# Adapter and expert FFN on one Trainium2 core: the opening reordered in two halves

## The reference

```
hidden = gelu(x @ down_W.T + down_b)                       # 512 -> 128
Wsel, bsel = expert_W[id0], expert_b[id0]
expert_out = hidden @ Wsel.T + bsel
hidden = where(valid, expert_out, hidden) + domain_emb[id0]
x1 = layernorm(hidden @ up_W.T + up_b + x) * ln_gamma + ln_beta
h = gelu(x1 @ Wi[id1] + bi[id1])                           # 512 -> 2048
y = layernorm(h @ Wo[id1] + bo[id1] + x1) * gamma[id1] + beta[id1]
```

## Time and profile before

| what | value |
|---|---|
| median of 3 runs | 781.45 us (781.15 to 781.71) |
| the profiled execution | 781.23 us |
| its span in the trace | 779.4 us |
| PE busy | 762.1 us, 98% |
| DVE, POOL, ACT busy | 516.7, 466.2, 347.4 us |
| DMA | 45.70 MB, mean 59 GB/s |
| PE busy from 60 us to the end | 707.52 of 719.40 us |

### The profile page before, as it was taken

How to read it: one execution, slowest core, us unless ns; L and a number is a source line. 1 busy time by engine, 2 the same in 40 slices (tenths; PEclk the granted TensorE clock), 3 DMA queues, 4 the chain that set the end, 5 groups by cost and what they waited for, 6 DMA issues and landing times.

```text
span 779.4 us, 10642 instructions
## 1 busy us (share of the span) xinstructions
PE 762.1 (98%) x3418; PEld 631.0 (81%) x3418; DVE 516.7 (66%) x1064; ACT 347.4 (45%) x601; POOL 466.2 (60%) x401
## 2 busy tenths in 40 slices
PE   8999999999999999999999999999999999999996
PEld 7878887888878888788887888878887888888885
DVE  6676874678556894578837798277874778646115
ACT  3454445434445344534445444444445434443432
POOL 5766654675647756386644855548654676646444
PEclk9999999999999999999999999999999999999999
DMA  9930000310012000137212200022000110001001
GB/s 325 407 126 1 1 0 1 122 41 0 1 56 82 27 1 1 70 115 276 81 55 68 95 0 1 3 95 68 1 1 1 64 45 1 0 12 43 1 0 54
DMA packets 17049, 45.70 MB, mean 59 GB/s; under 512 B 2274, under 2 KB 2530, under 8 KB 16098
## 3 DMA queue, kind: packets, MB, share of 16 engines
q1 hardware_dynamic: 16274, 43.67, 15.4%
q10 hardware_dynamic: 720, 1.31, 0.6%
HBM read 36.59 MB, written 8.39 MB: 58 GB/s over the span
## 4 chain that ended last, share of the span: by engine, by line
PE 91%; DVE 4%; issue 2%; ACT 1%; DMA 1%; POOL 0%; ACTq 0%; DVEq 0%; POOLq 0%
PE acc L751 15%; PE acc L753 15%; PE acc L752 14%; PE ps_h L751 14%; PE ps_h L753 14%; PE ps_h L752 14%; PE ps L751 2%; PE ps L753 2%; PE ps L752 2%; DVE xt L525 1%; DVE rows L607 1%; DMA xt_raw<-in_xT 1%; ACT ps_h L434 1%; PE ps_h L823 0%; DVE x1t L590 0%
## 5 line engine op out<-in xcount | busy, mean ns | idle before, releaser
L274 POOL TENSOR_TENSOR wi<-w_raw,wi 128x512 fp32r<-128x512 f32 x128 | 165.4, 1293 | 257.0 <-ACT wi L418 256.9
L433 ACT ACTIVATE h<-ps_h,bi_now 128x512 fp32r<-128x512 f32 x126 | 86.9, 690 | 372.3 <-PE ps_h L753 372.2
L595 DVE TENSOR_TENSOR h<-ps_h,h 128x512 fp32r<-128x512 f32 x126 | 87.0, 691 | 198.5 <-ACT ps_h L434 197.6
L751 PE MATMUL acc<-wo,h 128*128 128x512 f32 x512 | 199.2, 389 | 0.0
L752 PE MATMUL acc<-wo,h 128*128 128x512 f32 x512 | 199.2, 389 | 0.0
L753 PE MATMUL acc<-wo,h 128*128 128x512 f32 x512 | 199.2, 389 | 0.0
L751 PE MATMUL ps_h<-x1t,wi 128*128 128x512 f32 (+1 forms) x512 | 197.7, 386 | 0.4 <-DVE x1t L590 0.2
L752 PE MATMUL ps_h<-x1t,wi 128*128 128x512 f32 (+1 forms) x512 | 197.5, 386 | 0.0
L753 PE MATMUL ps_h<-x1t,wi 128*128 128x512 f32 (+1 forms) x512 | 197.5, 386 | 0.0
L280 POOL TENSOR_TENSOR wo<-w_raw,wo 128x512 fp32r<-128x512 f32 x128 | 165.9, 1297 | 7.1 <-ACT wo L424 7.1
L584 DVE STREAM_TRANSPOSE ps<-rows 32x128 f32<-32x128 f32 x448 | 144.2, 322 | 5.7
(11 more groups left out here) (129 smaller groups left out, 584.6 us busy)
## 6 DMA issues: line engine op xcount, KB each, us to landing
w_raw<-in_w SPq DMA_DIRECT2D x32, 512.0 KB, 8.5
rows<-in_x SPq DMA_DIRECT2D x32, 256.0 KB, 2.8
out<-rows SPq DMA_DIRECT2D x32, 256.0 KB, 2.0
xt_raw<-in_xT SPq DMA_DIRECT2D x7, 1024.0 KB, 4.8
vec<-in_vec SPq DMA_DIRECT2D x2, 768.0 KB, 10.7
xt_raw<-in_xT ACTq DMA_DIRECT2D x4, 256.0 KB, 6.1
vec<-in_vec SPq DMA_DIRECT2D x1, 512.0 KB, 6.6
down_raw<-in_down ACTq DMA_DIRECT2D x1, 256.5 KB, 2.7
```

The lines of the kernel that those rows point to most:

```text
L274: pool.tensor_tensor(slot[:, 1], w_raw[:, c, 0, :].rearrange("p (k i) -> p k i", k=KD), slot[:, 0].bitcast(F32), ALU.subtract).then_inc(wi ...
L433: act.activation(h[:, c % H_RING, 0, :], bank, ACT.Gelu, bias=bias)
L595: dve.tensor_tensor(h[:, c % H_RING, 1, :], hidden_bank(t, c), h[:, c % H_RING, 0, :].bitcast(F32), ALU.subtract).then_inc(h_split, 1)
L751: pe.matmul(out, left[0], right[0], start=start, stop=False)
```

## The change

Everything lies in the opening, but for one item (the fold of the second sequence).

- **Two halves.** `xt_raw` is loaded in four pieces j, each two chunks k of 256 columns (rows of x): j = 0, 1 are the first 256 rows, j = 2, 3 the last. Pieces 2 and 3 are issued after ACT's table load and first gelu. `first_down(j)` is 6 matmuls of 256 columns; j = 0, 1 go to `ps0` bank 0, j = 2, 3 to bank 1, later. `first_hidden` and `first_hid_rest` work on 256 columns. The rests of pieces 0 and 1 are DVE's (`first_rest`), those of 2 and 3 POOL's; so `xt_split`, on which SP waits before it issues the next tile's `xt_raw`, now comes from POOL.
- **Expert.** ACT makes the hi part (scale = valid), DVE the rest in one operation; identity * (1 - valid) is a matrix of its own (`exp_off`, kept in a corner of `fold_w`), and `fold_product` has 5 matmuls rather than 3, for both sequences. ACT makes `exp_b`. POOL computes `valid`. The fold of sequence 0 goes into a `ps_h` bank.
- **Down weights.** Both parts by DVE (before: DVE and POOL).
- **Residuals** of s = 0, 1 by one fp32 matmul each with the identity (`first_residual`); their norms one after the other rather than as a pair.
- **keep_warm** only once, 11 matmuls.
- **Order.** `first_down(2)`, `(3)` and two bias products stand before `turn(0)`; `adapter_up` of s = 2, 3 behind `turn(0)` and `turn(1)`. On POOL the four `wi_rest` come before the last two `inverse_root`; `add_out_bias(0)` moves into c = 1 to 4 of tile 0. The first two `xt_round`/`xt_rest` of tile 1 come before the first gelus. `vec0` is loaded before the first `w_raw`. The copy of `bi` for tile 0 is gone.

```diff
-WARM = (14, 1, 12, 6)
+WARM = 11
...
+        exp_off = [fold_w[:, b, 1, 0:A] for b in range(BATCH)]
...
+        def fold_bank(b):
+            return ps0[:, 1, :] if b else ps_h[:, 0, :]
+        def half(j):
+            return slice(j // 2 * HALF, (j // 2 + 1) * HALF)
+        def pair(j):
+            return slice(j % 2 * 2, j % 2 * 2 + 2)
...
+            sp.dma_start(vec0[:, :, :], vec0_d[:, 1:3, :].to_broadcast([P, 2, D])).then_inc(vec0_landed, 16)
             load_w(0, 0)
-            sp.dma_start(vec0[:, :, :], vec0_d[:, 1:3, :].to_broadcast([P, 2, D])).then_inc(vec0_landed, 16)
...
             pool.wait_ge(up_b_landed, 16)
-            for s in range(SUB):
-                add_up_bias(0, 1, s, 0)
+            add_up_bias(0, 1, 0, 0)
+            add_up_bias(0, 1, 1, 0)
+            first_rest(2)
+            first_rest(3)
             inverse_root(0, 0, 0)
+            add_up_bias(0, 1, 2, 0)
             inverse_root(0, 0, 1)
+            add_up_bias(0, 1, 3, 0)
             wi_rest(0, 0)
             wi_rest(0, 1)
+            wi_rest(0, 2)
+            wi_rest(0, 3)
             inverse_root(0, 0, 2)
             inverse_root(0, 0, 3)
-            wi_rest(0, 2)
-            wi_rest(0, 3)
...
-            for k in range(KD):
-                act.dma_start(xt_raw[:, k, :], xT_d[0, :, k, :]).then_inc(xt_first[k], 16)
+            for j in (0, 1):
+                act.dma_start(xt_raw[:, pair(j), half(j)], xT_d[0, :, pair(j), half(j)]).then_inc(xt_first[j], 16)
             act.wait_ge(const_ready, 2)
             act.activation(warm[:, :], neghalf[:, :], ACT.Gelu)
+            for j in (2, 3):
+                act.dma_start(xt_raw[:, pair(j), half(j)], xT_d[0, :, pair(j), half(j)]).then_inc(xt_first[j], 16)
...
+            first_round(0)
+            first_round(1)
             act.wait_ge(up_landed, 16)
             act.activation(up_w[:, 0, :], up_raw, ACT.Copy).then_inc(up_w_hi, 1)
-            act.wait_ge(down_landed, 16)
-            hidden(0)
+            expert_round()
+            first_expert_bias()
+            first_hidden(0, half_hi)
             fold_round(0)
+            first_round(2)
+            first_round(3)
             wi_round(0, 0, 0)
+            first_hidden(2, hid_hi)
             wi_round(0, 0, 1)
             x1t_round(0, 0, 0)
+            wi_round(0, 0, 2)
             x1t_round(0, 1, 0)
...
             x1t_round(0, 3, 0)
+            xt_round(1, 0)
+            xt_round(1, 1)
             for c in range(EARLY):
                 gelu(0, c, 0)
...
+            first_stats(0)
+            first_var(0)
             dve.wait_ge(vec0_landed, 16)
-            adapter_rows(0, (0, 1), 0, acc_part)
+            first_center(0)
+            first_stats(1)
+            first_scale(0)
+            first_var(1)
+            first_center(1)
+            first_hid_rest(2, hid_hi, hid_split)
+            first_scale(1)
             adapter_sum(0, 2, 0, acc_part(2))
...
+            def first_residual(s):
+                pe.wait_ge(xb_ready, s + 1)
+                pe.matmul(acc[:, s, :], ident[:, :], rows[:, 0, s, :], start=False, stop=False)
...
-                three(ps0[:, 1, :], [exp_w[:, i, :] for i in (0, 1)], [up_w[:, i, :] for i in (0, 1)],
-                      True, True).then_inc(fold_done, 1)
+                three(fold_bank(b), [exp_w[:, i, :] for i in (0, 1)], [up_w[:, i, :] for i in (0, 1)], True, False)
+                pe.matmul(fold_bank(b), exp_off[b], up_w[:, 0, :], start=False, stop=False)
+                pe.matmul(fold_bank(b), exp_off[b], up_w[:, 1, :], start=False, stop=True).then_inc(fold_done, 1)
...
-            keep_warm(WARM[0], ps_h[:, 1, :])
+            keep_warm(WARM, ps_h[:, 1, :])
             pe.wait_ge(down_w_ready, 1)
-            for k in range(KD):
-                adapter_down(0, k)
-            keep_warm(WARM[1], ps_h[:, 1, :])
+            first_down(0)
+            first_down(1)
             fold_product(0)
...
-            keep_warm(WARM[2], ps_h[:, 1, :])
+            first_down(2)
+            first_down(3)
+            bias_product(0, acc[:, 2, :], alone=False)
+            bias_product(0, acc[:, 3, :], alone=False)
             turn(0)
+            adapter_up(0, 0, 2, acc[:, 2, :], alone=False)
             turn(1)
-            keep_warm(WARM[3], ps_h[:, 1, :])
+            adapter_up(0, 0, 3, acc[:, 3, :], alone=False)
```

More of the change, by code:

```diff
@@ L328, in _ @@
[L328 to L332, removed]
+            pool.wait_ge(ids_all_landed, 16)
+            step(pool.tensor_scalar(valid[:, 0, :], ids_all[:, :], 0.0, None, ALU.is_ge))
+            step(pool.tensor_scalar(valid[:, 1, :], ids_all[:, :], float(E0), None, ALU.is_lt))
@@ new lines, in _, with first_rest @@
+            step(pool.tensor_tensor(valid[:, 0, :], valid[:, 0, :], valid[:, 1, :], ALU.mult))
+            step(pool.tensor_scalar(valid[:, 1, :], valid[:, 0, :], -1.0, 1.0, ALU.mult, ALU.add))
+            pool.sem_inc(valid_ready, 1)
+            pool.tensor_scalar(exp_off[0], ident[:, :], valid[:, 1, 0:1], None, ALU.mult).then_inc(exp_off_ready, 1)
+            def first_rest(j):
+                pool.wait_ge(xt_hi, j + 1)
+                part = x1t[1][:, :, pair(j), half(j)]
+                pool.tensor_tensor(part[:, 1], xt_raw[:, pair(j), half(j)], part[:, 0].bitcast(F32),
+                                   ALU.subtract).then_inc(xt_split, 1)
@@ L426, in gelu @@
             def gelu(t, c, parity):
-                if c == 0:
-                    act.wait_ge(bi_now_ready, t + 1)
+                first = isinstance(t, int) and t == 0
+                if c == 0 and first:
+                    act.wait_ge(bi_landed[0], 16)
+                elif c == 0:
+                    act.wait_ge(bi_now_ready, t)
                 act.wait_ge(mm1_done, CH * t + c + 1)
-                bias = bi_now[:, parity, c:c + 1]
+                bias = bi[:, 0, c:c + 1] if first else bi_now[:, parity, c:c + 1]
                 bank = hidden_bank(t, c)
@@ L460, in tile @@
                         x1t_round(t + 1, SPLIT_AT.index(c), 1 - parity)
-                    if more and c in (0, 1):
+                    if more and c in (0, 1) and not (isinstance(t, int) and t == 0 and c == 0):
                         xt_round(t + 1, 2 * c)
@@ L658, in expert_bias @@
                 dve.tensor_tensor(exp_b[:, 1, :], wide, exp_b[:, 0, :].bitcast(F32), ALU.subtract).then_inc(exp_b_ready, 1)
[L661 to L665, removed]
-            dve.wait_ge(down_landed, 16)
-            dve.tensor_copy(down_w[:, 0, :, :], chunks(down_raw[:, 0:D])).then_inc(down_w_hi, 1)
-            for k in range(KD):
-                xt_rest(0, k)
+            dve.wait_ge(down_landed, 16)
+            step(dve.tensor_copy(down_w[:, 0, :, :], chunks(down_raw[:, :])))
+            dve.tensor_tensor(down_w[:, 1, :, :], chunks(down_raw[:, :]), down_w[:, 0, :, :].bitcast(F32),
+                              ALU.subtract).then_inc(down_w_ready, 1)
+            first_rest(0)
+            first_rest(1)
             dve.wait_ge(up_w_hi, 1)
             dve.tensor_tensor(up_w[:, 1, :], up_raw, up_w[:, 0, :].bitcast(F32), ALU.subtract).then_inc(up_w_ready, 1)
-            dve.wait_ge(valid_ready, 1)
-            expert_bias(0)
-            hid_rest(0)
+            dve.wait_ge(exp_hi, 1)
+            expert_rest(0)
+            dve.wait_ge(first_split, 2)
+            dve.sem_inc(xt_split, 2)
+            first_hid_rest(0, half_hi, half_split)
             fold_rest(0)
```

152 lines of the change are left out of this document (103 added, 49 removed).

## The result

The changed kernel takes 777.32 us (median of 6 runs, 776.74 to 777.95) against 781.58 us (6 runs, 780.7 to 781.77): ratio 0.9946, 95% interval 0.9936 to 0.9956. The forecast was 776.9 and "faster". The profiled execution took 776.74 us with a span of 774.9, 4.5 under the 779.4 of before: the sum of the prediction to the tenth. Some of that is luck, as this execution is the fastest of its six; the medians are 4.26 us apart.

A forecast was written before the change was run, and what follows sets the result against it. PE's own work bounds the kernel from 60 us on, a latency chain the opening; 3.85 + 1.1 - 0.46 = 4.5 us off the profiled 781.23 gives 776.7, at the median 776.9. Own range 776.0 to 777.9; 80% range 775.8 to 779.6.

The forecast's parts named there:

- To the fold: Opening up to sequence 0's fold: PE begins at 6.6 us, `exp_w` is ready at 10.0, the fold runs to 11.4.
- First two subtiles: Adapter products of subtiles 0 and 1 after the fold: residual matmul 0.95 us each, subtile 1 done at 16.1.
- a price of nothing: POOL's rests of pieces 2 and 3, from 13.1 to 15.6 us, cost nothing because PE is still on subtile 1.
- Turns and start: Transposes and first FFN products: early products at 22.15 us, second halves at 29.2 instead of 33.05, a gain of 3.85.
- the stall for `wi_rest`: PE's wait for POOL's third `wi_rest` in the opening; done at 23.6 us, wanted at 25.05, so the stall goes.
- Behind it: After the opening: tile 1's first two `xt_rest` ahead of the gelus remove PE's stall at 44.02, worth 1.1 us.
- Given back: The second fold has two matmuls more on PE's path, which costs 0.46 us.
- tight but inside: POOL's added operations in c = 1 to 4 of tile 0: 5.1 us against 5.5 us of PE, so they fit.
- The clock did fall: Rival: PE's clock is low when real work starts, slow to 13 us; gain 1.5 us, time 780; 15%.
- the third rival: With fewer fillers the clock falls or stays down through the whole adapter: 9 us lost, time 786; 6%.
- The second half was not late: Rival: the second half or DVE comes later, 2 us late giving a gain of 2.5 to 3, time 778.7; 12%.
- no weight held the products: Rival: late weights hold the first FFN products, so there is no change, 781 to 782; 5%.

The follow-up runs named there:

- a_dve_rest: Changed kernel with the rests of pieces 2 and 3 of x on DVE instead of POOL: 777.41 us, 0.9948 of the kernel before.
- the two order experiments: POOL's last two `wi_rest` put ahead of the last two roots in the kernel before (779.79 us), and back behind them in the changed kernel (779.58 us).
- b_xt_early: Kernel before with only tile 1's first two `xt_round`/`xt_rest` moved ahead of tile 0's first gelus: 781.52 us, ratio 1.0002.
- a_fold1: Changed kernel with the second sequence's fold as before (three matmuls, identity part added by DVE): 782.52 us, 1.0023 of the kernel before.
- a_xt_late: Changed kernel with tile 1's first two roundings and rests put back behind the gelus: 778.27 us, 0.996 of the kernel before.
- a_wi_order: Changed kernel with POOL's last two `wi_rest` put back behind the last two roots: 779.58 us, 0.9973 of the kernel before.
- a_warm10: Changed kernel with 10 filler matmuls instead of 11, nothing else: 783.63 us, 1.0023 of the kernel before.
- a_fold1_pad: Changed kernel with the second fold as before (as in a_fold1) and 12 fillers instead of 11: 785.01 us, 1.0042 of the kernel before.
- a_warm0: Changed kernel without any filler matmuls: 777.96 us, 0.9955 of the kernel before.
- a_both: Changed kernel with the shorter second fold, 14 fillers and tile 0's `add_out_bias` moved ahead of the tile loop: 776.48 us, 0.9937 of the kernel before.

## Why the prediction was right, step by step

- **To the fold.** Piece 1 landed at 7.70 (forecast 7.73), piece 0 only at 6.24 instead of 5.24. So PE began at 7.74, not 6.6, and its long idle stretch (1.11 us) lies ahead of its first product, not behind it; the chain does not go through it. The two unknown 128x128 steps, taken as 0.3 each, took 0.41 and 0.36. `exp_w` was ready at 10.3, forecast 10.0. This is nearly all of the error in the opening.
- **First two subtiles.** The plain fp32 residual, bounded by 0.23 and 1.0 and taken as 0.95, took 0.98 and 0.86 in the chain. The upper bound was the right neighbour: the same kind of matmul. Subtile 1 ended at 16.36 (16.1). POOL's rests of pieces 2 and 3 ended at 15.9, ahead of that, as said, and a_dve_rest confirms a price of nothing. The Trainium skill (GPSIMD Engine Reference, Performance versus the Vector engine) speaks for VectorE here; it did not decide, although its ratio held (2.51 for POOL's two, 1.28 for DVE's two in a_dve_rest).
- **Turns and start.** The first turn began at 19.03 (18.8), the second was over by 20.52 (20.4), start at 22.30 (22.15), the last scale ended at 27.20 (27.15), second halves at 29.33 (29.2). The gain there is 3.7, forecast 3.85. Of it 2.05 is the earlier start and 1.65 the stall for `wi_rest`, which the two order experiments measured from both sides (1.64 and 1.68). The halves themselves, with the expert's new operations, were not undone by themselves: that they give the earlier start is read from the marks of the chain, and of the parts only the residual matmuls (0.7) and the fillers (1.0) were measured.
- **Behind it.** The early rests of tile 1 were put at 1.1; undoing them cost 1.16. My reason, an idle engine, was right, but the engine is idle only because POOL's additions and the copy of `bi` had moved away (b_xt_early). The prediction added these parts as if each stood alone.
- **Given back.** Two fold matmuls 0.45 (0.46). SP issued tile 1's x at 15.96 (15.6), and ACT took it at 28.45 without a wait. The four `add_out_bias` between the chunks made no wait of PE, but used up DVE's slack: "tight but inside" was right by less than one operation of 1.3 us (a_fold1).
- **The rivals.** The clock did fall, between 8 and 14 us, in the profiled runs of five of the variants (a_xt_late, a_wi_order, a_dve_rest, a_warm10, a_fold1_pad). Their starts were 0.8, 0.8, 1.3, 0.9 and 2.1 us later than 22.30, not 3; the 2.1 is not the clock's alone, since piece 0 landed only at 7.50 there. In these five PE idled 1.33 to 2.08 us ahead of its first product, in the runs with fillers that kept the clock at most 1.11. The changed kernel's own runs differ by 1.2 us, those with 14 fillers by 0.5; that this is the clock is argued from their mean clocks (0.996 in three slower ones, 0.998 in the others) and was not read in their traces, and the kernel before, timed beside it, differs by 1.1 as well. PE did not lose its clock at the turns, where the third rival had it: 1.00 from 12 us on in the changed kernel. The second half was not late, and no weight held the products.
- **Not foreseen.** That the number of instructions in the opening decides whether the loop stands still. The changed kernel is at the first number that is free of it, and that is luck: no term of the sum has it. Four instructions less (a_warm10) would have made the forecast of "faster" wrong.

## What to carry to other kernels

Where latency sets a stretch, write down the chain step by step with durations from the nearest rows of the same kind; errors of up to 0.3 us a step stay small (the one of 1.0 us here, piece 0, fell beside the chain), and the shift can then be checked at three or four marks. Do not add the gains of parts that use the same engine's idle time before each has been tried without the others. When an edit that removes work makes a later loop slower and the profile names only "issue", look at the packets of the instruction queue and count the engine's instructions ahead of the loop before blaming the work itself; a filler or two may place the loop better.

## What the runs showed of the hardware that was not expected

- PE's instructions come in 16 KB packets, 14 or 32 of them for the same work, and a border right behind this loop's start costs 2.0 to 2.9 us at each of the two jumps back, plus slow matmuls after it.
- VectorE's short operations on SBUF last as long as one of POOL's (1.2 to 1.4 us, even for one element a lane) while POOL works without a pause, and 0.23 to 0.29 in its pauses (a_fold1, a_both); rests that read PSUM keep 0.69. The Trainium skill (SBUF — State Buffer, SBUF: two separate sides) describes the port that the two share as an exclusive lock for a whole instruction; the traces agree.
- In a_xt_late PE idled 1.39 us ahead of its first product, at 7.51, and the granted clock read 0.72 and then 0.50 until 12 us; in the changed kernel it idled 1.11 us there, at 7.74, and the clock stayed at 1.00. The row isn't the pace itself: in a_warm0 it reads 1.00 from 8 to 12 us while the matmuls go at half pace until 12.6, and in a_both 0.94 to 0.95 from 6 us to the end with 512 columns 0.23 apart as ever.
